# Layer one's convolution: pairs of heads against two bands at once, and running sums in place of averages

## What is computed

```python
avg = cumsum(h, axis=1) / arange(1, l + 1)[None, :, None]      # running average over the tokens
ci = avg.reshape(b, l, H, d).transpose(0, 2, 1, 3).reshape(b * H, l, d)
pc = ci @ W_pe + b_pe                                          # 62 numbers a token and head
dyn, gate = pc[..., :K], pc[..., K:]
w = softmax(stt + sigmoid(gate) * dyn)                         # 31 weights a token and head
w = where(t_idx + k_idx - (K - 1) >= 0, w, 0)
for kk in range(K):                                            # causal convolution of ci by w
    out = out + w[:, :, kk:kk+1] * padded[:, kk:kk+l, :]
v = layernorm(conv_loc @ W_fc.T + h) * gamma + beta
```

## Time and profile before

| | us |
|---|---|
| three timed runs, median (lowest, highest) | 3874.67 (3867.59, 3876.83) |
| the profiled execution, its own time | 3875.27 |
| its span from the first to the last instruction | 3873.5 |
| PE busy in the span | 3402.5 (88%) |
| DVE busy | 2855.6 (74%) |
| ACT busy | 1948.4 (50%) |
| POOL busy | 1272.1 (33%) |

### The profile page before, as it was taken

The page is one execution under the profiler, slowest core; times in us unless marked ns, Lnnn a source line. Parts: engine busy times, 40 slices in busy tenths (PEclk is TensorE's granted clock), DMA queues, the critical chain, the costliest instruction groups (busy, mean ns, idle before and its releaser), DMA issues.

```text
span 3873.5 us, 70678 instructions
## 1 busy us (share of the span) xinstructions
PE 3402.5 (88%) x27050; PEld 2837.9 (73%) x27050; DVE 2855.6 (74%) x6364; ACT 1948.4 (50%) x3778; POOL 1272.1 (33%) x1014
## 2 busy tenths in 40 slices
PE   4999999999951199999999726999999999999999
PEld 2888888888841188888888715777777777777787
DVE  4677777777757877777777258788888888878864
ACT  2666666666630055555554424555555555555544
POOL 1233333333220045556555433222222222223210
PEclk7999999999975599999999958999999999999999
DMA  4132322222120223333333246555555555555551
GB/s 180 61 102 97 103 99 96 75 80 74 46 65 0 44 73 73 78 85 89 80 72 77 35 106 125 109 116 118 119 118 117 120 122 119 120 118 120 104 102 39
DMA packets 741209, 355.90 MB, mean 92 GB/s; under 512 B 549500, under 2 KB 694248, under 8 KB 740744
## 3 DMA queue, kind: packets, MB, share of 16 engines
q1 hardware_dynamic: 716296, 316.76, 33.3%
q0 software_dynamic: 24576, 34.62, 5.2%
HBM read 215.37 MB, written 135.92 MB: 91 GB/s over the span
## 4 chain that ended last, share of the span: by engine, by line
PE 74%; DVE 14%; issue 4%; ACT 4%; POOL 1%; DMA 1%; SPq 1%; POOLq 0%; another core or an unknown queue 0%; ACTq 0%; DVEq 0%
PE bank L1207 9%; PE bank L1223 8%; PE bank L1795 8%; PE bank L750 8%; PE bank L731 8%; PE bank L1781 8%; PE bank L1753 6%; PE bank L116 5%; PE bank L709 3%; PE bank L1764 2%; DVE hits L1040 2%; PE bank L1735 2%; ACT xh_ L500 2%; PE bank L1190 1%; DVE w L1643 1%
## 5 line engine op out<-in xcount | busy, mean ns | idle before, releaser
L1479 POOL TENSOR_TENSOR energies<-energies,energy 128x496 f32<-128x496 f32 x128 | 173.5, 1356 | 743.1 <-DVE energies L1624 743.1
L988 ACT ACTIVATE bank<-bank,fc_bias 128x512 f32<-128x512 f32 x256 | 169.5, 662 | 407.9 <-PE bank L1207 407.3
L1149 DVE TENSOR_TENSOR hidden_low<-bank,hidden_high 128x512 fp32r<-128x512 f32 x256 | 174.1, 690 | 270.1 <-ACT hidden_high L994 266.6
L1795 PE MATMUL bank<-l_w_high,l_hidden_low 128*128 128x256 f32 x1024 | 310.9, 304 | 52.8 <-DVE l_hidden_low L1687 52.7
L639 DVE TENSOR_TENSOR gT_low<-bank,gT_high 128x512 fp32r<-128x512 f32 x256 | 173.4, 688 | 228.7 <-ACT gT_high L545 228.7
L1128 DVE TENSOR_TENSOR onehot_p<-bank,slot_p 128x1024 bf16<-128x1024 f32 x256 | 311.0, 1215 | 0.0
L750 PE MATMUL bank<-w_high,gT_low 128*128 128x256 f32 x1024 | 308.4, 301 | 0.8 <-DVE gT_low L639 0.8
L539 ACT ACTIVATE bank<-bank,b 128x512 f32<-128x512 f32 x256 | 170.1, 664 | 273.4 <-PE bank L731 270.5
L1687 DVE TENSOR_TENSOR l_hidden_low<-bank,l_hidden_high 128x512 fp32r<-128x512 f32 x256 | 172.9, 686 | 173.7 <-ACT l_hidden_high L1563 173.5
L1795 PE MATMUL bank<-l_w_high,l_hidden_high 128*128 128x256 f32 x1024 | 289.8, 283 | 0.0
L750 PE MATMUL bank<-w_high,gT_high 128*128 128x256 f32 x1024 | 289.2, 282 | 0.0
(11 more groups left out here) (302 smaller groups left out, 11012.7 us busy)
## 6 DMA issues: line engine op xcount, KB each, us to landing
bandT<-bands SPq DMA_DIRECT2D x352, 240.0 KB, 3.6
fc_full<-in_L_ffn_fc_wT SPq DMA_DIRECT2D x32, 1024.0 KB, 4.9
bands<-zeros SPq DMA_DIRECT2D x22, 768.0 KB, 8.6
x<-in_L_attn_x SPq DMA_DIRECT2D x32, 512.0 KB, 6.3
moe_output<-zeros SPq DMA_DIRECT2D x32, 512.0 KB, 7.2
x_after_retention<-x SPq DMA_DIRECT2D x32, 512.0 KB, 3.0
moe_input_and_gates<-xn SPq DMA_DIRECT2D x32, 512.0 KB, 4.1
x<-x_after_retention SPq DMA_DIRECT2D x32, 512.0 KB, 4.1
```

Of the source, the lines that this page charges most:

```text
L1149: v.tensor_tensor(t.hidden.low[:, n % SLICES, :], K.banks[t.bank["expand", i, g, 0]][:, :], t.hidden.high[:, n % SLICES, :], ALU.subtract) ...
L1479: e.tensor_tensor(e1[:, :, :], e1[:, :, :], t.energy[:, :, :], ALU.add).then_inc(s("full_energy"), 1)
L1795: p = pe.matmul(K.banks[6 + ch // 2][:, left:left + D], x, w, start=False, stop=f == KF - 1 and j == 2 and ch % 2 == 1)
```

## The change

The convolution loads the 32 channels of a pair of heads together, as one stationary block without zeros, and sends both heads' bands past it in one matmul of 192 columns. Half of the result is wanted (the even head's channels from the even band, the odd head's from the odd band): ACT copies the even band's part, multiplied by a per-partition 1 or 0 (`parity`), and a new DVE step `select` adds the odd band's part, multiplied by 0 or 1. `convT` is signalled by `select`. Running sums `sumT` take the place of the averages: DVE's multiplication by one over the count goes away, the bias matmul runs against the counts in place of ones, ACT's tanh takes half of one over the count as its scale, a second ACT instruction makes (tanh + 1) / count, `gated` becomes a plain product, and the copy to `window` divides by the count. The places of nearly all steps of layer one are new, and so is the hold time of the convolution's bank. Cut to its core:

```diff
 PLACES_D = {
-    "l1_contract": 2.44, ... "norm_in": (8.51, 16.43), "load_bias_row": 15.47, ... "add_row": (18.24, 22.24),
+    "l1_contract": 2.17, ... "norm_in": (7.91, 15.83), "load_bias_row": 17.77, ... "add_row": (17.77, 22.28),
-    "kernel_product": (20.22, 21.64, 23.06, 24.48, 25.9, 27.32, 28.74, 30.16), "gated": (20.45, 21.87, 23.29, 24.71, 26.13, 27.55, 28.97, 30.39),
-    "energies": (20.92, 22.33, 23.76, 25.18, 26.6, 28.02, 29.44, 30.86),
+    "kernel_product": (20.22, 21.68, 23.1, 24.52, 25.94, 27.36, 28.78, 30.2), "gated": (20.28, 21.7, 23.12, 24.54, 25.96, 27.38, 28.8, 30.02),
+    "energies": (21.09, 22.5, 24.22, 25.56, 26.77, 28.19, 29.61, 31.03),
-    "softmax": (21.62, 23.04, 24.46, 25.88, 27.3, 28.72, 30.14, 31.56),
+    "softmax": (21.63, 23.05, 24.47, 25.89, 27.31, 28.73, 29.9, 31.57),
-    "convolve": (33.0, 34.15, 35.31, 36.46, 37.61, 38.76, 39.91, 41.06, 42.21, 43.36, 44.51),
+    "convolve": (33.04, 34.19, 35.35, 36.5, 37.65, 38.8, 40.13, 41.1, 42.25, 43.4, 44.55),
+    "select": (33.37, 34.52, 35.68, 36.83, 37.98, 38.78, 40.17, 41.43, 42.58, 43.73, 44.88),
-    "mix": (34.93, 36.09, 37.24, 39.54, 40.69, 41.84, 44.14, 45.29), "center_mid": (34.98, 36.13, 37.28, 39.58, 40.73, 41.88, 43.96, 45.33),
+    "mix": (35.47, 36.63, 37.78, 40.13, 41.23, 42.38, 44.68, 45.83), "center_mid": (35.47, 36.62, 37.77, 40.07, 41.22, 42.37, 44.45, 45.82),
-    "root_mid": (40.53, 45.61), "residual_mid": (39.77, 45.57), "stats_x3": (41.43, 47.23), ...
+    "root_mid": (41.02, 46.1), "residual_mid": (40.26, 47.03), "stats_x3": (41.62, 47.2), ...
-    "turn_mid": (45.63, 50.89), "load_out_row": 50.48, "gain_out": (57.78, 65.78), "result": (58.77, 66.77),
+    "turn_mid": (45.81, 51.03), "load_out_row": 49.69, "gain_out": (57.19, 65.3), "result": (58.66, 66.46),
 }
-BANKS_D = {... "convolve": (1, 0.4), ...}
+BANKS_D = {... "convolve": (1, 0.9), ...}
...
+    t.b1, t.counts = K.tile(ctx, "l1_b1", [P, KF]), K.tile(ctx, "counts", [P, S], F32R)
+    t.per_count, t.half_per_count = K.tile(ctx, "per_count", [P, C]), K.tile(ctx, "half_per_count", [P, C])
+    t.per_window, t.parity = K.tile(ctx, "per_window", [P, K.NT]), K.tile(ctx, "parity", [P, 2])
-    t.window = K.ring(ctx, "window", 2, [P, H // 2, 2, 2 * t.HD])
+    t.window = K.ring(ctx, "window", 2, [P, D])
-    t.loads = 16 * (10 + P // t.HD)
+    t.loads = 16 * (13 + P // t.HD)
...
 # layer_one_pool
-    e.memset(t.window[0][:, :, :, :], 0.0)
-    e.memset(t.window[1][:, :, :, :], 0.0).then_inc(s("pool_setup"), 1)
...
 # layer_one_scalar
-            e.activation(t.th[n % 2][:, :, :], kernel_view(K, t, b, ch, 1), ACT.Tanh, scale=0.5).then_inc(s("gate"), 1)
+            e.activation(t.th[n % 2][:, :, :], kernel_view(K, t, b, ch, 1), ACT.Tanh, scale=t.half_per_count[:, ch:ch + 1]).then_inc(s("tanh"), 1)
+            e.wait_ge(s("tanh"), n + 1)
+            e.activation(t.th[n % 2][:, :, :], t.th[n % 2][:, :, :], ACT.Identity, scale=t.per_count[:, ch:ch + 1],
+                         bias=t.per_count[:, ch:ch + 1]).then_inc(s("gate"), 1)
...
-            e.copy(out, src).then_inc(s("window"), 1)
+            e.activation(t.window[n % 2][:, :], K.banks[t.bank["window_turn", b, *args, 0]][:, 0:D], ACT.Copy,
+                         scale=t.per_window[:, args[0]:args[0] + 1]).then_inc(s("window"), 1)
...
-            e.copy(t.convT[:, :, place:place + size],
-                   K.banks[t.bank["convolve", b, i, 0]][:, 0:KD * TT].rearrange("p (k t) -> p k t", k=KD)[:, :, 0:size]).then_inc(s("convT"), 1)
+            e.activation(t.convT[:, :, place:place + size], conv_view(K, t, b, i, 0, size), ACT.Copy, scale=t.parity[:, 0:1]).then_inc(s("conv_even"), 1)
...
+def conv_view(K, t, b, i, odd, size):
+    return K.banks[t.bank["convolve", b, i, 0]][:, 0:K.KD * 2 * K.TT].rearrange("p (k o t) -> p k o t", k=K.KD, o=2)[:, :, odd, 0:size]
...
 # layer_one_vector
+    v.tensor_copy(t.counts[:, :], t.counts_full)
+    v.tensor_scalar(t.half_per_count[:, :], t.per_count[:, :], 0.5, None, ALU.mult)
...
-            v.tensor_tensor_scan(view, ...).then_inc(step, c.up())
-            v.wait_ge(step, c.n)
-            v.tensor_tensor(view, view, t.per_count[:, :], ALU.mult).then_inc(s("avgT"), 1)
+            v.tensor_tensor_scan(view, ...).then_inc(s("sumT"), 1)
...
-            v.scalar_tensor_tensor(out=e1..., in0=t.th[n % 2][:, :, :], scalar=1.0, in1=kernel_view(K, t, b, ch, 0), op0=ALU.add, op1=ALU.mult)
+            v.tensor_tensor(e1..., t.th[n % 2][:, :, :], kernel_view(K, t, b, ch, 0), ALU.mult)
...
+        elif name == "select":
+            (i,) = args
+            n, size, place = b * NT + i, min(K.TT, S - i * K.TT), i * K.TT % t.CIRCLE
+            v.wait_ge(s("conv_even"), n + 1)
+            out = t.convT[:, :, place:place + size]
+            v.scalar_tensor_tensor(out=out, in0=conv_view(K, t, b, i, 1, size), scalar=t.parity[:, 1:2], in1=out, op0=ALU.mult, op1=ALU.add).then_inc(s("convT"), 1)
...
 # layer_one_tensor, kernel_product
-                pe.matmul(pair[r][:, 0:4 * t.RW], t.ones[rows, :], t.pe_bias[...], start=True, stop=False)
+                pe.matmul(pair[r][:, 0:4 * t.RW], t.counts[rows, ch * P:(ch + 1) * P], t.pe_bias[...], start=True, stop=False)
...
 # layer_one_tensor, convolve
             for k in range(KD):
-                for odd in range(2):
-                    for g in range(4):
-                        pair = 4 * k + g
-                        m = pe.matmul(bank[32 * g:32 * (g + 1), k * TT:(k + 1) * TT], t.window[n % 2][:, pair, odd, :],
-                                      t.bandT[n % 2][:, :, g // 2 * H // 2 + k * t.HR + g % 2 * 2 + odd], start=odd == 0, stop=odd == 1)
+                for g in range(4):
+                    cols, head = slice(32 * g, 32 * (g + 1)), g // 2 * H // 2 + k * t.HR + g % 2 * 2
+                    m = pe.matmul(bank[cols, k * 2 * TT:(k + 1) * 2 * TT], t.window[n % 2][:, k * P + 32 * g:k * P + 32 * (g + 1)],
+                                  t.bandT[n % 2][:, :, head:head + 2].rearrange("p t o -> p o t"), start=True, stop=True)
```

More of the change, by code:

```diff
@@ L33 @@
     + [f"slot_i{n}" for n in range(4)] + ["gates"] + [f"l1_mlp_low{n}" for n in range(4)] + ["rows_split"],
[L34 removed]
+    "pool": ["ident_zero", "ident", "zeros", "bias_zero", "gate_energy", "w_pe_zero", "pads0", "pads1", "bands"],
 }
@@ L1230 @@
 PLACES_D = {
-    "l1_contract": 2.44, "load": (3.0, 10.8), "join": (5.44, 13.37), "stats_in": (6.76, 14.66), "root_in": (7.74, 15.64), "norm_in": (8.51, 16.43),
-    "load_bias_row": 15.47, "turn_in": (16.83, 17.43), "average": (17.92, 18.45), "add_row": (18.24, 22.24),
-    "kernel_product": (20.22, 21.64, 23.06, 24.48, 25.9, 27.32, 28.74, 30.16), "gated": (20.45, 21.87, 23.29, 24.71, 26.13, 27.55, 28.97, 30.39),
-    "energies": (20.92, 22.33, 23.76, 25.18, 26.6, 28.02, 29.44, 30.86), "exponentials": (21.21, 22.63, 24.05, 25.47, 26.89, 28.31, 29.73, 31.15),
@@ new lines @@
+    "energies": (21.09, 22.5, 24.22, 25.56, 26.77, 28.19, 29.61, 31.03), "exponentials": (21.38, 22.8, 24.22, 25.64, 27.06, 28.48, 29.9, 31.32),
+    "softmax": (21.63, 23.05, 24.47, 25.89, 27.31, 28.73, 29.9, 31.57), "first_bands": 24.76, "load_gain_row": 31.27,
+    "window_turn": (32.44, 33.59, 34.74, 35.9, 37.05, 38.2, 39.35, 40.5, 41.65, 42.8, 42.85),
+    "convolve": (33.04, 34.19, 35.35, 36.5, 37.65, 38.8, 40.13, 41.1, 42.25, 43.4, 44.55),
+    "select": (33.37, 34.52, 35.68, 36.83, 37.98, 38.78, 40.17, 41.43, 42.58, 43.73, 44.88),
@@ L1729, in layer_one_tensor @@
                 rows = slice(r * P // 2, (r + 1) * P // 2)
-                pe.matmul(pair[r][:, 0:4 * t.RW], t.ones[rows, :], t.pe_bias[rows, :, :, :, :].rearrange("o a j q k -> o (a j q k)"), start=True, stop=False)
+                pe.matmul(pair[r][:, 0:4 * t.RW], t.counts[rows, ch * P:(ch + 1) * P], t.pe_bias[rows, :, :, :, :].rearrange("o a j q k -> o (a j q k)"), start=True, stop=False)
             for j in range(KD):
@@ L1734, in layer_one_tensor @@
                     out = pair[r][:, 0:4 * t.RW].rearrange("p (a j c) -> p j a c", a=2, j=KD)[:, j, :, :]
-                    m = pe.matmul(out, t.avgT[b % 2][rows, j, PAD + ch * P:PAD + (ch + 1) * P],
+                    m = pe.matmul(out, t.sumT[b % 2][rows, j, PAD + ch * P:PAD + (ch + 1) * P],
                                   t.w_pe[rows, :, :, :].rearrange("p a q k -> p (a q k)"), start=False, stop=j == KD - 1)
```

45 lines of the change are left out of this document (24 added, 21 removed).

## The result

The changed kernel takes **3912.3 us** (median of 4 runs, 3910.2 to 3916.1), the kernel before 3874.8 beside it: ratio 1.0101, 95% interval 1.0084 to 1.0119. The change costs 1%, 37 us; the forecast was 3870, no change.

The account below looks back on a forecast made before the run. PE sets the pace: a batch is some 90 us of PE, 4 waiting for DVE, up to 1.7 of slow clock. 3875.3 - 4 (matmuls) + 0 + 0 = 3871, said as 3870; range 3798 to 3920.

Parts of the forecast that it names:

- one of your cases: At contractions 9 and 14 and mix 4 and 5: PE comes to wait for DVE, +42 us, 3917; chance 0.25.

Follow-up runs that it names:

- the two tries at products 3 and 7: Changed kernel with layer one's banks given by a search, 3965.8 us; changed kernel with new places for mix and center_mid alone, 4010.4 us.
- the places' 13 us: Kernel before with the changed kernel's table of places and nothing else of the change: 3886.7 us, ratio 1.0033.

## What to carry to other kernels

Before merging matmuls, ask what a round is made of: time the same columns in fewer records at two clocks or, better, with neighbours side by side. Here records were free, columns dear for lying 64 bytes apart, and changing the order of two indices was worth 60 us where halving the records was worth nothing. In a kernel whose banks come from a table, a hold is not a guard that costs nothing: work the whole plan through with the new constant and see which step gets whose bank. The slack on paper is not the price, though: the product with -0.21 never waited and the one with +0.11 waited 1.2 us in every batch. So read the waits step by step in the trace before repairing one; the two tries at products 3 and 7 were aimed at the wrong ones. And a total that comes out as one of your cases had it is no evidence for that case until its waits stand where it put them.

## What the hardware showed beside

DVE and GpSimd slow each other. Timeline of the changed kernel, where the new places put two additions of 1024 columns side by side:
```profile
3105.88 3.97 POOL L1472 TENSOR_TENSOR x<-x,row_bias 128x1024 f32<-128x1024 f32 x1 [8.04 <-DMA row_bias<-rows_layer]
...
3107.57 3.36 DVE L1717 TENSOR_TENSOR x<-x,o 128x1024 f32<-128x1024 f32 x1
```
Apart from each other the same two took 2.41 and 1.22 us (at 3122.88 and 3062.18 us of the same trace): 3.6 us of work that here lasts from 3105.88 to 3110.93, 5.1 us. Between 2500 and 3700 us L1717 took 2248 ns in the mean (1217 in the median, so some of them only), the same addition before the change 1219. The Trainium skill (Advanced Engine Details and Errata, "GPSIMD Details") has GpSimd share an interface with DVE instructions that read two SBUF inputs; by that rule these two collide and a plan should keep them apart; the trace agrees with its 3.36 us for 1.22. Whether this is part of the places' 13 us wasn't tried.
